# In-degree count of a two-layer graph network: one-hots from a constant row and one number per partition instead of two broadcast tensors

## What is computed

```python
# layer 0, twice (hidden 256 with relu, then 128)
h    = x @ W
deg  = segment_sum(ones(E), dst, num_segments=50000) + 1.0
dinv = rsqrt(deg)
agg  = segment_sum(h[src] * (dinv[src] * dinv[dst])[:, None], dst) + h * (dinv * dinv)[:, None]
# layer 1: gated messages, segment_sum over dst, a GRU cell, batch norm over the nodes
x = layernorm(x + layer0(x)); x = layernorm(x + layer1(x))
```

## Time and profile before

| what | value |
|---|---|
| median of 3 runs | 1928.1 us (1924.65 to 1928.97) |
| the profiled execution | 1930.21 us, span 1928.5 us |
| mean granted PE clock of the profiled execution | 0.929 of full speed |
| busy, share of the span | PE 1583.2 us (82%), PEld 1103.0 (57%), DVE 1369.0 (71%), ACT 1231.8 (64%), POOL 945.6 (49%) |
| instructions | PE 8258, DVE 4573, ACT 3127, POOL 911 |

### The profile page before, as it was taken

How to read it: one execution, slowest core, us unless ns; L and a number is a source line. 1 busy time by engine, 2 the same in 40 slices (tenths; PEclk the granted TensorE clock), 3 DMA queues, 4 the chain that set the end, 5 groups by cost and what they waited for, 6 DMA issues and landing times.

```text
span 1928.5 us, 36544 instructions
## 1 busy us (share of the span) xinstructions
PE 1583.2 (82%) x8258; PEld 1103.0 (57%) x8258; DVE 1369.0 (71%) x4573; ACT 1231.8 (64%) x3127; POOL 945.6 (49%) x911
## 2 busy tenths in 40 slices
PE   5400599999999957999998986999999999976664
PEld 2200387788778845777776764555555555545543
DVE  7916366676666645666666663688888888878897
ACT  0385366666666624666666665677777777757788
POOL 5000566666666636666666662666666666600000
PEclk8855799999999987999999998999999999987898
DMA  8496466653444434777766665687775444439987
GB/s 260 165 340 260 151 191 189 191 175 132 137 137 137 137 120 152 256 251 256 250 201 194 198 200 173 189 227 231 230 210 142 127 126 133 124 111 354 347 282 245
DMA packets 218927, 382.40 MB, mean 198 GB/s; under 512 B 38959, under 2 KB 41228, under 8 KB 218832
## 3 DMA queue, kind: packets, MB, share of 16 engines
q1 hardware_dynamic: 190272, 342.01, 52.4%
q0 software_dynamic: 28560, 39.34, 10.1%
HBM read 222.75 MB, written 177.81 MB: 208 GB/s over the span
## 4 chain that ended last, share of the span: by engine, by line
PE 70%; DVE 11%; issue 7%; DMA 6%; ACT 3%; POOL 1%; SPq 1%; DVEq 1%; another core or an unknown queue 1%; POOLq 0%; ACTq 0%
PE bank L1332 10%; PE bank L1315 9%; PE bank L1307 9%; PE bank L1299 5%; PE bank L1382 5%; PE bank L1368 4%; PE bank L1370 4%; PE bank L1375 4%; PE bank L1374 4%; PE bank L1372 4%; PE bank L1351 3%; DVE gath L1207 3%; PE bank L1354 3%; DVE onehot L1084 2%; PE bank L1294 2%
## 5 line engine op out<-in xcount | busy, mean ns | idle before, releaser
L668 POOL DMA_INDIRECT gath<-XP,ROWI x294 | 298.0, 1014 | 335.0 <-issue 229.7
L668 POOL DMA_INDIRECT gath<-MT,ROWI x294 | 325.7, 1108 | 205.7 <-PE bank L1382 106.6
L668 POOL DMA_INDIRECT gath<-G,ROWI x294 | 294.8, 1003 | 193.7 <-PE bank L1332 96.5
L1332 PE MATMUL bank<-gath,onehot 128*128 128x128 f32 x1176 | 164.2, 292 | 71.6 <-issue 30.8
L1315 PEld LDWEIGHTS bank<-w_sb,page 128*128 128x128 f32 x1568 | 191.0, 192 | 49.3 <-issue 49.3
L740 ACT ACTIVATE page<-bank,b_sb 128x512 f32<-128x512 f32 x196 | 124.1, 684 | 112.3 <-PE bank L1307 90.3
L1315 PE MATMUL bank<-w_sb,page 128*128 128x128 f32 x1568 | 192.0, 275 | 1.7 <-issue 1.7
L1332 PEld LDWEIGHTS bank<-gath,onehot 128*128 128x128 f32 x1176 | 146.0, 200 | 79.2 <-issue 65.0
L1307 PE MATMUL bank<-page,w_sb 128*128 128x512 f32 x392 | 185.7, 596 | 1.6 <-issue 1.6
L1402 PE MATMUL bank<-ident,page 128*128 128x128 f32 x784 | 125.3, 308 | 73.2 <-DMA page<-YT 66.2
L1051 DVE TENSOR_TENSOR page<-bank,DINV 128x512 f32<-128x512 f32 x98 | 67.8, 692 | 155.3 <-PE bank L1315 142.0
(11 more groups left out here) (213 smaller groups left out, 3562.4 us busy)
## 6 DMA issues: line engine op xcount, KB each, us to landing
page<-YT SPq DMA_DIRECT2D x196, 256.0 KB, 4.1
MT<-page SPq DMA_DIRECT2D x98, 260.0 KB
XP<-page SPq DMA_DIRECT2D x98, 256.0 KB, 2.1
G<-page SPq DMA_DIRECT2D x98, 256.0 KB
OWN<-page SPq DMA_DIRECT2D x98, 256.0 KB
page<-OWN SPq DMA_DIRECT2D x98, 256.0 KB
YT<-page SPq DMA_DIRECT2D x98, 256.0 KB
page<-AD SPq DMA_DIRECT2D x98, 256.0 KB
```

Of the source, the lines that this page charges most:

```text
L668: nc.gpsimd.indirect_dma_start(gath[k][:, w, 0:width], None, rows, bass.IndirectOffsetOnAxis(ap=ROWI[:, at:at + 1], axis=0), bounds_check= ...
L1332: last = nc.tensor.matmul(bank[k][:, j * D:(j + 1) * D], onehot[k][:, first:first + P], gath[g.slot(4)][:, w, 0:D], start=(i == 0), stop=( ...
```

## The change

Each one-hot of a chunk is now an instruction of its own: `tensor_scalar` with the constant row `tile_h` as its only tensor and one number per partition (a column of `lo_f` or `hi_f`) as a scalar operand read through a pointer. So 2 x 196 = 392 instructions of 128 or 392 elements per partition take the place of 50 of 1024 or 3136 (the last two of half that size). The batches, the slots, the semaphores and the order of everything else on DVE stay. Further:

- `tile_h` has 392 elements per partition; `col_h` had 784. POOL writes it at the same place of its program.
- `hi_f` and `lo_f` are f32 instead of f16, the constants stay f16 and the one-hots bf16.
- A chunk's one-hots lie side by side in memory now; before, the elements of two chunks alternated, so PE read every second element. PE's 196 products and their shapes are unchanged.

```diff
-PAIRS = 4
+CHUNKS = 8
-BATCHES = ET // (2 * PAIRS)
-REST = ET // 2 - BATCHES * PAIRS
+BATCHES = ET // CHUNKS
+REST = ET - BATCHES * CHUNKS
...
-        hi_f, lo_f = (rows.bitcast(F16)[:, 0:ET].rearrange("p (n b) -> p n b", b=2) for rows in (spare[2], spare[2][:, ET:]))
+        hi_f, lo_f = spare[2][:, 0:ET], spare[2][:, ET:2 * ET]
...
-        col_h = early("col_h", [P, NT, 2], F16)
+        tile_h = early("tile_h", [P, NT], F16)
-        oh_lo = early("oh_lo", [P, OH_SLOTS, PAIRS, P, 2], BF16)
-        oh_hi = early("oh_hi", [P, OH_SLOTS, PAIRS, NT, 2], BF16)
+        oh_lo = early("oh_lo", [P, OH_SLOTS, CHUNKS, P], BF16)
+        oh_hi = early("oh_hi", [P, OH_SLOTS, CHUNKS, NT], BF16)
...
-            nc.gpsimd.iota(col_h[:], [[1, NT], [0, 2]], base=0, channel_multiplier=0, **exact).then_inc(consts, 1)
+            nc.gpsimd.iota(tile_h[:], [[1, NT]], base=0, channel_multiplier=0, **exact).then_inc(consts, 1)
...
             def one_hots(n):
-                slot, at, pairs = n % OH_SLOTS, n * PAIRS, PAIRS if n < BATCHES else REST
+                slot, chunks = n % OH_SLOTS, CHUNKS if n < BATCHES else REST
                 wait(dve, oh_used, n + 1 - OH_SLOTS)
-
-                def one_hot_pairs(made, parts, width):
-                    return nc.vector.tensor_tensor(made[:, slot, 0:pairs], col_h[:, 0:width, :].unsqueeze(1).to_broadcast([P, pairs, width, 2]),
-                                                   parts[:, at:at + pairs, :].unsqueeze(2).to_broadcast([P, pairs, width, 2]), ALU.is_equal)
-
-                one_hot_pairs(oh_lo, lo_f, P)
-                one_hot_pairs(oh_hi, hi_f, NT).then_inc(oh_ready, 1)
+                for c in range(chunks):
+                    at = n * CHUNKS + c
+                    nc.vector.tensor_scalar(oh_lo[:, slot, c, :], tile_h[:, 0:P], lo_f[:, at:at + 1], None, ALU.is_equal)
+                    last = nc.vector.tensor_scalar(oh_hi[:, slot, c, :], tile_h[:], hi_f[:, at:at + 1], None, ALU.is_equal)
+                last.then_inc(oh_ready, 1)
...
-                for b in range(pairs):
-                    for c in range(2):
-                        last = nc.tensor.matmul(bank[0][:, 0:NT], oh_lo[:, slot, b, :, c], oh_hi[:, slot, b, :, c],
+                for c in range(chunks):
+                    last = nc.tensor.matmul(bank[0][:, 0:NT], oh_lo[:, slot, c, :], oh_hi[:, slot, c, :],
```

More of the change, by code:

```diff
@@ L321, in build_gnn @@
         bm_row = early("bm_row", [P, D])
-        col_h = early("col_h", [P, NT, 2], F16)
+        tile_h = early("tile_h", [P, NT], F16)
         wa_sb = early("wa_sb", [P, D])
         waT_sb = early("waT_sb", [P, D])
-        oh_lo = early("oh_lo", [P, OH_SLOTS, PAIRS, P, 2], BF16)
-        oh_hi = early("oh_hi", [P, OH_SLOTS, PAIRS, NT, 2], BF16)
-        after_lo = oh_lo[:].rearrange("p s n c b -> p (s n c b)").bitcast(F32)
-        after_hi = oh_hi[:].rearrange("p s n c b -> p (s n c b)").bitcast(F32)
+        oh_lo = early("oh_lo", [P, OH_SLOTS, CHUNKS, P], BF16)
+        oh_hi = early("oh_hi", [P, OH_SLOTS, CHUNKS, NT], BF16)
+        after_lo = oh_lo[:].rearrange("p s n c -> p (s n c)").bitcast(F32)
+        after_hi = oh_hi[:].rearrange("p s n c -> p (s n c)").bitcast(F32)
         win_t, win_u = (after_lo[:, at:at + W * P].rearrange("p (w e) -> p w e", w=W).bitcast(I32) for at in (0, W * P))
@@ L877, in _ @@
             link(nc.vector.tensor_scalar(lo_i[:], dst_e[:], P - 1, None, ALU.bitwise_and))
-            nc.vector.tensor_copy(hi_f.rearrange("p n b -> p (n b)"), hi_i[:])
-            link(nc.vector.tensor_copy(lo_f.rearrange("p n b -> p (n b)"), lo_i[:]))
+            nc.vector.tensor_copy(hi_f, hi_i[:])
+            link(nc.vector.tensor_copy(lo_f, lo_i[:]))
             dve.wait_ge(consts, CONSTS)
             def one_hots(n):
-                slot, at, pairs = n % OH_SLOTS, n * PAIRS, PAIRS if n < BATCHES else REST
+                slot, chunks = n % OH_SLOTS, CHUNKS if n < BATCHES else REST
                 wait(dve, oh_used, n + 1 - OH_SLOTS)
-                def one_hot_pairs(made, parts, width):
-                    return nc.vector.tensor_tensor(made[:, slot, 0:pairs], col_h[:, 0:width, :].unsqueeze(1).to_broadcast([P, pairs, width, 2]),
-                                                   parts[:, at:at + pairs, :].unsqueeze(2).to_broadcast([P, pairs, width, 2]), ALU.is_equal)
-                one_hot_pairs(oh_lo, lo_f, P)
-                one_hot_pairs(oh_hi, hi_f, NT).then_inc(oh_ready, 1)
+                for c in range(chunks):
[3 more added lines that the diff above has]
+                last.then_inc(oh_ready, 1)
             one_hots(0)
@@ L1247, in _ @@
             for n in range(BATCHES + 1):
-                slot, pairs = n % OH_SLOTS, PAIRS if n < BATCHES else REST
+                slot, chunks = n % OH_SLOTS, CHUNKS if n < BATCHES else REST
                 pe.wait_ge(oh_ready, n + 1)
-                for b in range(pairs):
-                    for c in range(2):
-                        last = nc.tensor.matmul(bank[0][:, 0:NT], oh_lo[:, slot, b, :, c], oh_hi[:, slot, b, :, c],
-                                                start=n == 0 and b + c == 0, stop=n == BATCHES and b == pairs - 1 and c == 1,
-                                                skip_group_check=True)
+                for c in range(chunks):
+                    last = nc.tensor.matmul(bank[0][:, 0:NT], oh_lo[:, slot, c, :], oh_hi[:, slot, c, :],
+                                            start=n == 0 and c == 0, stop=n == BATCHES and c == chunks - 1, skip_group_check=True)
                 last.then_inc(oh_used, 1)
```

## The result

| | before | changed |
|---|---|---|
| median of 7 runs each | 1924.65 us | 1936.85 us |
| range | 1922.74 to 1928.97 | 1933.17 to 1940.98 |
| profiled execution, span | 1928.5 us | 1936.0 us |

The changed kernel is slower: ratio 1.0058, 95% interval 1.0045 to 1.0071, or +11.2 us (+8.7 to +13.7). The three runs shown ahead of the prediction had a median of 1928.1 us; of seven it is 1924.65, so 3.5 us of the distance between forecast (1944.1) and measurement (1936.85) is the reference, and the rest is the sum: +16 forecast, +11 to +12 measured.

A forecast was written before the change was run, and what follows sets the result against it. DVE's pace in the count was taken to bound the kernel: 15.1 us later count end, 0.6 PE tail and 0.3 POOL gathers make +16 us on 1930.2; with the median 2.1 lower, 1944.1 us, range 1937 to 1958.

The forecast's parts named there:

- What bounds, and that all of it counts: Count at the kernel's start: DVE sets the pace, and each microsecond the count ends later is one of the kernel.
- The price of a pointer instruction: DVE one-hots in the count: 0.133 us fixed per instruction, about 0.065 us of it for reading the number.
- The fixed price of the Trainium skill: DVE instructions in SBUF: 58 cycles fixed, estimated 0.06 us each, no pointer extra; by it the change would gain.
- The rate per element: DVE one-hots in the count: 16-bit operands and a single tensor combine their halvings, to 0.26 ns per element.
- The other rival: DVE one-hots: the two halvings don't combine, 0.52 ns per element, count end +38.5 + 0.9 us, 1967.5 us; chance 0.10.
- Batches 3 to 24: Main part of the count on DVE: 172 chunks at 0.401 us, 69.0 us, ending at 89.3 instead of 74.2.
- The start of batch 3: DVE after the c_row gathers: 20.3 instead of 23.80 us (19.0 to 22.4), a gain taken as 3.5 us.
- The tail and POOL's gathers: Count's end on PE: +0.6 us from a possibly lower clock; six window gathers beside batches 3 to 10: +0.3 us.
- The first (the pointer read is hidden): DVE one-hots in the count: 0.07 us fixed per instruction, 0.275 us a chunk, -5 us, 1923 us; chance 0.08.
- the third: Count: something gives most of the loss back, price near 0.09 us per instruction and best start gain, 1928 us; chance 0.03.

The follow-up runs named there:

- all three changes: Kernel before with its table written by two POOL instructions, batches 3 to 7 made before the gather wait, dst split at 256: 1909.41 us beside 1926.29, ratio 0.991.

## Why the prediction was right and where it was wrong

**What bounds, and that all of it counts.** Right. The count came 11.97 us later, ACT began 11.97 us later, the medians differ by 12.2 us. In seven of the eight experiments the interval of the total holds the shift of the time at which the counts are read, from -16 to +37 us; with constants the total fell by 12 us (9 to 14) and the count by 8.25, and those 4 us stay open.

**The price of a pointer instruction.** Right, and it decided the sign. Taken as 0.133 us from lines 1008 and 904; 0.16 and 0.24 us between starts, less 0.033 and 0.102 us for elements, leave 0.127 and 0.138, and the 3.15 us of a batch give 0.13 each. A batch was forecast at 3.21 us and took 3.15. The part that the pointer adds was forecast as 0.065 us; it is 0.061.

**The fixed price of the Trainium skill** (VectorE: DVE Perf Modes, The TRN2 errata), 58 cycles or an estimated 0.06 us, holds for what reads no pointer: with constants in the instructions 0.137 us a chunk remain beside the elements, 0.07 each. For the instructions of this change the measurement decides, 0.13 us each, and with it the sign.

**The rate per element.** Right: 0.26 ns, shown by taking it away. The other rival, 0.52 ns, was priced at +39 us; the kernel with the f32 row, which has that rate, measured +37 us in the count and +36 in the total.

**Batches 3 to 24.** 67.8 us instead of 69.0: -1.2 us, from the 0.06 us per batch.

**The start of batch 3 is the step that failed**, by its size: "So batch 3 starts at 20.3 instead of 23.80 us (19.0 to 22.4)". It started at 18.50, outside my bounds. Batch 0 began at 4.84 instead of 5.9 us: DVE's small preparations between `ended` and batch 0, whose length I took from rows in which POOL was working beside them, took 0.9 us (3.91 to 4.84) instead of 1.4, `ended` began 0.3 us sooner, and POOL's constants were there at 3.82 us. The rows of the kernel before from which the 1.4 us came:

```profile
6.16 0.34 DVE L876 TENSOR_SCALAR gath<-gath 128x196 int32<-128x196 int32 x1
...
7.33 0.25 DVE L879 CAST gath<-gath 128x196 f16<-128x196 int32 x1
```

So the first gather came 2.5 us earlier, not 1.4. The third gather then began 2.9 us behind the first (8.54 to 11.45) instead of 6.0 (11.04 to 17.02), a gain of 3.1 us where I had taken 2.1; it took 0.3 us longer itself (1.27 instead of 0.97). 2.5 + 3.1 - 0.3 = 5.3 us instead of 3.5. The rows had the pattern of the wait (a gather ends its usual 0.9 us behind a long DVE instruction), and I gave it too little weight. -1.8 us.

**The tail and POOL's gathers.** +0.9 forecast, -0.2 measured. I took the granted clock as half lowered by PE's longer idle times; it was 1.00 at the end, as the rows of the changed kernel show, and the tail was 0.93 us instead of 1.13. The 0.2 us less have a plain cause that I had not looked at: in the kernel before PE was still at the batch before when DVE ended at 74.2 us (it had begun it at 73.00), while in the changed kernel it was just done with it (84.81 + 1.50 = 86.31 us, DVE's end 86.33). The worry was not empty: with the f32 row the clock did fall, and the tail was 1.53 us. My 2.6 us for a batch at the lower clock was too little as well, it took 2.80, which DVE's 3.15 still hid. DVE's period beside POOL's window gathers was not longer by anything that shows in the sum.

So 16.0 - 1.2 - 1.8 - 1.1 = 11.9 us. **The range** (1937 to 1958) began 0.15 us above the measured median. Of the distance, 4 us are these terms and 3.5 us the reference, which three runs had put at 1928.1 and seven put at 1924.65: I subtracted nothing for that, though the three runs themselves spanned 4.3 us. The range should have held the spread of the reference as well.

**The rivals.** None came true. The first (the pointer read is hidden) is refuted by the batch of 3.15 us where it needed 2.2, and the second (0.52 ns) by the same number, where it needed 4.3. The kernel with constants shows what the first would have brought: it forecast -5 us, and the counts come 8.25 us earlier; the 3 us between are the start of batch 3, 17.3 us instead of the 20.3 that I had forecast. Nothing gave most of the loss back, so the third fell too.

## What to carry to other kernels

Before a wide instruction is split into many narrow ones, count both parts of the price: elements times rate, and the fixed part, with 0.06 us more for each number that is read per partition. Here twice the rate halved the 2.17 us of elements per batch (to 1.08), and 16 instructions at 0.13 us instead of 2 at 0.07 took back 1.9 us. An estimate from these numbers: a form with a pointer pays only above some 256 elements per instruction, where the 0.26 ns saved per element outweigh the 0.067 us more per instruction, and above some 500 where one wide instruction is cut into many, so that the whole 0.13 us is new. And look at what an engine waits for beside its main loop: a table pattern, an order and a split that nobody had asked about were worth 16 us together, more than the change cost.

## What the runs showed of the hardware that was not expected

- POOL's iota with an inner run of 2 took 4.39 us for 784 elements, two iotas of 392 at a step of 2 took 0.57 us each, one of 392 in a row 0.46.
- A `tensor_scalar` of 294 elements that overlaps POOL's long iota waits for all of it: `ended` took 2.35 us beside it (2.71 with the old table added, where it began earlier) and 0.42 without. The other way round, POOL's first two gathers took 3.0 and 2.3 us beside DVE instructions of 1.78 us and 1.1 to 1.2 us beside instructions of 0.3 us. The Trainium skill has such a rule (SBUF — State Buffer, SBUF: two separate sides): where DVE's instruction uses both of its ports, or reads two tensors in SBUF against a GpSimd operation that reads SBUF too, the one that starts first holds the shared pair of ports for its whole instruction and the other waits. The durations above agree with that, and show that many short instructions let the other engine in soon.
- One gather goes beyond that rule. The first gather of the windows, in the kernel before and in the one with all three changes:

```profile
24.17 5.15 POOL L654 DMA_INDIRECT win_src<-in_src,start_i  x1 [6.19 <-DVE start_i L906]
...
24.99 33.96 POOL L657 DMA_INDIRECT win_src<-in_src,start_i  x1 [11.72 <-DVE start_i L909]
```

  It lasted until about 0.85 us behind DVE's next pause, not behind its next instruction: DVE paused at 28.5 us in the kernel before, and not before the end of the count, 58.1 us, with all three. It took 1.00 us beside the short instructions of the changed kernel. Why this gather and not those behind it (1 to 2 us) is open. It cost nothing here: the last window gather ended at 65.3 us and DVE read the windows from 67.23 us on, but whoever removes the last pause of DVE should look at what POOL has to issue.
- The granted clock of PE stayed at its upper level (2.4 GHz) from 31 us on in the changed kernel, with PE at work for 1.50 us of every 3.15. With the f32 row, at 1.50 to 2.79 us of every 4.24, it went up and down between the levels.
- Twice as many products of half the columns, each with its own weights, took PE hardly longer at the upper clock: 1.58 us for 16 of 196 columns, 1.56 us for 8 of 392 in the kernel before.
